# Two residual layers on 32 batches: small products in another order, sums of x on VectorE, sums of weights issued early on GpSimd

## What is computed

```python
def L0(x, weight, bias, lora_a, lora_b, scaling, adapter_id):
    base = jnp.einsum('bsi,oi->bso', x, weight) + bias
    low = jnp.einsum('bsi,bri->bsr', x, lora_a[adapter_id])
    return base + scaling[adapter_id][:, None, None] * jnp.einsum('bsr,bor->bso', low, lora_b[adapter_id])

def L1(x, weight, adapter_ids):
    return jnp.einsum('bij,bkj->bik', x, weight[adapter_ids])

x = x + L0(x, ...)      # x (32, 128, 2048), weight (2048, 2048)
x = x + L1(x, ...)      # weight (16, 2048, 2048), one of 14 used by each batch
```

## Time and profile before

| | |
|---|---|
| median of 3 runs | 2782.98 us (2781.64 to 2783.62) |
| the profiled execution, its own time | 2777.48 us |
| its span in the profile | 2775.7 us |
| mean granted clock of TensorE | 0.972 |
| TensorE busy in matmuls | 2603.3 us (94% of the span) |
| VectorE busy | 2257.2 us (81%) |
| ScalarE busy | 1392.5 us (50%) |
| GpSimd busy | 1100.5 us (40%) |
| plain DMA queue | 649.46 MB, 65.4% of 16 engines |
| accumulating DMA queue | 33.56 MB, 6.4% |

### The profile page before, as it was taken

How to read it: one execution, slowest core, us unless ns; L and a number is a source line. 1 busy time by engine, 2 the same in 40 slices (tenths; PEclk the granted TensorE clock), 3 DMA queues, 4 the chain that set the end, 5 groups by cost and what they waited for, 6 DMA issues and landing times.

```text
span 2775.7 us, 35408 instructions
## 1 busy us (share of the span) xinstructions
PE 2603.3 (94%) x12154; PEld 2132.6 (77%) x12154; DVE 2257.2 (81%) x1902; ACT 1392.5 (50%) x1486; POOL 1100.5 (40%) x718
## 2 busy tenths in 40 slices
PE   7886998899998989998999999999999999999999
PEld 5665787677877777776888888888878878878887
DVE  7877799998887899887878888777877877867865
ACT  3322333333433333335666666666666756756665
POOL 7647477764446687551032041130320311301402
PEclk9998999999999999999999999999999999999999
DMA  5786764354366544656877768768799999998996
GB/s 217 303 298 233 227 182 137 116 187 167 122 206 212 176 134 167 191 207 240 287 259 277 266 222 309 243 237 284 248 351 325 334 352 338 321 349 302 312 320 234
DMA packets 213715, 686.32 MB, mean 247 GB/s; under 512 B 23424, under 2 KB 31648, under 8 KB 213536
## 3 DMA queue, kind: packets, MB, share of 16 engines
q1 hardware_dynamic: 204032, 649.46, 65.4%
q0 software_dynamic: 9216, 33.56, 6.4%
q10 hardware_dynamic: 288, 1.05, 0.1%
HBM read 650.42 MB, written 100.66 MB: 271 GB/s over the span
## 4 chain that ended last, share of the span: by engine, by line
PE 66%; DVE 16%; DMA 7%; issue 6%; POOL 3%; SPq 1%; ACT 1%; DVEq 0%; POOLq 0%; ACTq 0%
PE acc L1195 16%; PE acc L1196 16%; PE acc L1197 16%; PE acc L1112 6%; PE acc L1114 6%; PE acc L1113 6%; DVE tx L1067 5%; DVE ws L1067 5%; DVE xb L987 3%; DMA wb<-w 2%; DVE acc L1057 2%; DMA xb<-x_sums 2%; DMA xb<-x 1%; PE acc L1151 1%; DMA acc<-w 1%
## 5 line engine op out<-in xcount | busy, mean ns | idle before, releaser
L1067 DVE TENSOR_TENSOR ws<-wb,ws 128x1024 fp32r<-128x1024 f32 x964 | 1312.0, 1389 | 300.8 <-ACT ws L923 288.0
L923 ACT CAST ws<-wb 128x1024 fp32r<-128x1024 f32 x964 | 985.9, 1050 | 992.6 <-PE acc L1197 421.8
L1195 PE MATMUL acc<-ws,ops 128*128 128x512 f32 (+1 forms) x2048 | 804.2, 393 | 30.7 <-DVE lows L1017 17.8
L1196 PE MATMUL acc<-ws,ops 128*128 128x512 f32 (+1 forms) x2048 | 800.9, 391 | 0.0
L1197 PE MATMUL acc<-ws,ops 128*128 128x512 f32 (+1 forms) x2048 | 800.1, 391 | 0.0
L829 POOL TENSOR_TENSOR wb<-wb,eye_s 128x128 f32<-128x128 f32 x384 | 316.9, 855 | 1206.2 <-DMA wb<-w 1205.9
L1112 PE MATMUL acc<-tx,ws 128*128 128x512 f32 x1568 | 635.7, 405 | 132.7 <-DVE tx L1067 66.5
L1113 PE MATMUL acc<-tx,ws 128*128 128x512 f32 x1568 | 627.2, 400 | 0.0
L1114 PE MATMUL acc<-tx,ws 128*128 128x512 f32 x1568 | 627.0, 400 | 0.0
L1112 PEld LDWEIGHTS acc<-tx,ws 128*128 128x128 f32 x1568 | 305.6, 195 | 218.2 <-DVE tx L1067 80.5
L1195 PEld LDWEIGHTS acc<-ws,ops 128*128 128x128 f32 x2048 | 386.7, 189 | 112.1 <-DVE lows L1017 19.1
(11 more groups left out here) (64 smaller groups left out, 1249.4 us busy)
## 6 DMA issues: line engine op xcount, KB each, us to landing
wb<-w SPq DMA_DIRECT2D x816, 512.0 KB, 7.7
xb<-x SPq DMA_DIRECT2D x78, 512.0 KB, 5.5
wb<-w_sums SPq DMA_DIRECT2D x64, 512.0 KB, 7.0
xb<-x POOLq DMA_DIRECT2D x64, 512.0 KB, 8.7
y<-acc SPq DMA_DIRECT2D x32, 1024.0 KB, 8.1
out<-ost SPq DMA_DIRECT2D x128, 256.0 KB, 7.3
xst<-xt SPq DMA_DIRECT2D x60, 512.0 KB, 6.6
ystage<-y SPq DMA_DIRECT2D x60, 512.0 KB, 11.0
```

Source lines behind the costliest of these rows:

```text
L923: eng.copy(hi, src).then_inc(s_hi, 1)
L1067: eng.tensor_tensor(lo, src, hi, ALU.subtract).then_inc(s_lo, 1)
L1195: eng.matmul(dst, yh, wh, start=begin, stop=False)
L1196: eng.matmul(dst, yh, wl, start=False, stop=False)
```

## The change

The steps of a product come in another order. By the table `T_SLOT` the x operands are now b11, b21, t2, t1, t3 (in b12), b22 and t4 (in b21), and the second step is the plain product of b21 and a12. All four x sums are VectorE's (t3 = b22 - b12 is issued two steps before the product begins, t2 = b11 + t3 one step before, t4 and t1 in steps 0 and 1), and GpSimd keeps the weight sums: s1 = a21 + a22 is issued in the last two steps of the product before, s2 = s1 - a11 in steps 0 and 1, s4 and s3 behind. b21 and a12, which were used last, are now the operands of the second step; they are still the last blocks that come free in the product before. Evictions of a step are all issued at its end, z and w go to VectorE. Of the four sums of big weight blocks only two remain in DRAM (one VectorE operation per tile, 16 in all); products 3, 4 and 5 get their weights by an accumulating DMA ("wacc"), like x. Identity is added in four products of seven, not six. The LA blocks stand two steps earlier. The number of matmuls is the same.

```diff
-X_NEXT = {"b11": "b22", "b12": "b12", "b22": "b21", "b21": "b11"}
-W_NEXT = {"a11": "a21", "a21": "a11", "a22": "a12", "a12": "a22"}
-X_FREE = {"b11": 3, "b12": 4, "b22": 5, "b21": 6}
-W_FREE = {"a11": 3, "a21": 4, "a22": 5, "a12": 6}
-T_SLOT = ("b11", "b11", "b11", "b22", "b12", "b21", "b11")
-W_SLOT = ("a11", "a21", "a21", "a21", "a11", "a12", "a22")
+X_NEXT = {"b22": "b11", "b12": "b12", "b11": "b22", "b21": "b21"}
+W_NEXT = {"a21": "a21", "a22": "a11", "a11": "a12", "a12": "a22"}
+X_FREE = {"b22": 3, "b12": 4, "b11": 5, "b21": 6}
+W_FREE = {"a21": 3, "a22": 4, "a11": 5, "a12": 6}
+T_SLOT = ("b11", "b21", "b11", "b11", "b12", "b22", "b21")
+W_SLOT = ("a11", "a12", "a11", "a21", "a11", "a12", "a22")
...
-W_PLAIN = {0: (0, 0), 1: (0, 1), 6: (1, 1)}
-W_SUM = {2: 0, 3: 1, 4: 2, 5: 3}
-UNIT = (1, 0, -1, 2, 1, 2, 1)
+W_PLAIN = (("w", 0, 0), ("w", 0, 1), ("d", 0), ("d", 0), ("w", 0, 0), ("d", 0), ("w", 1, 1))
+W_ADDED = {3: ("w", 0, 0), 4: ("w", 1, 0), 5: ("d", 1)}
+UNIT = (1, 0, -1, 0, 1, 0, 1)
...
-        return te[at["W", s, ot]] + 0.5
+        return te[at["W", s, 3]] + 0.4 + 0.1 * ot
...
+        if n in W_ADDED:
+            for role in W_ROLE:
+                for h in range(2):
+                    adds.append((lo_key("W", s0 - K + W_FREE[role], h) + 9.0, "wacc", (q, role, h)))
         for h in range(2):
-            adds.append((lo_key("W", s0, h) + 1.3, "s3", (q, h)))
-            adds.append((lo_key("W", s0, h) + 4.0, "s1", (q, h)))
-            adds.append((lo_key("W", s0 + 1, h) + 1.3, "s2", (q, h)))
-            adds.append((lo_key("W", s0 + 2, h) + 1.3, "s4", (q, h)))
+            adds.append((past(s0 - 2 + h, 0.3) if q else -8.5 + 4.0 * h, "s1", (q, h)))
+            adds.append((past(s0 + h, 0.3) if q else lo_key("W", 0, h) + 8.0, "s2", (q, h)))
+            adds.append((past(s0 + 1 + h, 3.0 if h == 0 else 2.9), "s4", (q, h)))
+            adds.append((past(s0 + 2 + h, 0.3), "s3", (q, h)))
         for c in range(2):
-            sums1.append((lo_key("T", s0, c) + 2.0, "t1", (q, c)))
-            sums2.append((lo_key("T", s0 + 1, c) + 2.0, "t2", (q, c)))
-            adds.append((lo_key("T", s0 + 1, c) + 5.0, "t3", (q, c)))
-            adds.append((lo_key("T", s0 + 2, c) + 4.0, "t4", (q, c)))
+            sums.append((past(s0 - 2, 8.0 + 0.1 * c) if q else -12.0 + c, "t3", (q, c)))
+            sums.append((past(s0 - 1, 8.0 + 0.1 * c) if q else -9.0 + c, "t2", (q, c)))
+            sums.append((past(s0, 8.0 + 0.1 * c), "t4", (q, c)))
+            sums.append((past(s0 + 1, 8.0 + 0.1 * c), "t1", (q, c)))
...
+                if kind == "wacc":
+                    q, role, h = index
+                    eng.wait_ge(s_wb[WS[q][role]][h], 16 * (q + 1))
+                    eng.dma_start(w_tile(q, role, h), w_source(eng, q, role, h, W_ADDED[q % K]),
+                                  accum_op=ALU.add).then_inc(s_wa[WS[q][role]][h], 16)
+                    continue
...
+                    if what == "t3":
+                        x_saved(eng, q, "b12", c)
+                        x_ready(eng, q, "b12", c)
+                        x_ready(eng, q, "b22", c)
+                        ins = eng.tensor_tensor(b12, b22, b12, ALU.subtract)
+                    elif what == "t2":
+                        eng.wait_ge(s_lo, number["T", K * q, c] + 1)
+                        eng.wait_ge(s_sum, sum_no["t3", q, c])
                         x_saved(eng, q, "b11", c)
-                        x_ready(eng, q, "b12", c)
...
+                        ins = eng.tensor_tensor(b11, b11, b12, ALU.add)
```

More of the change, by code:

```diff
@@ L69, in slots_of @@
     return slots
[L72 removed]
+XS = [slots_of(("b11", "b12", "b21", "b22"), X_NEXT, q) for q in range(NG * K)]
 WS = [slots_of(("a11", "a12", "a21", "a22"), W_NEXT, q) for q in range(NG * K)]
@@ L235, in program, with past @@
         raw_user[k], free_at[k] = what, key + 1.5
-    adds, sums1, sums2 = [], [], []
+    def past(s, after):
+        return max(t_of(s), -12.0) + after
+    adds, sums = [], []
     for q in range(NG * K):
```

312 lines of the change are left out of this document (141 added, 171 removed).

## The result

| | before | after |
|---|---|---|
| median of the runs (us) | 2781.68 (2775.8 to 2783.62, 8 runs) | 2766.12 (2762.2 to 2772.58, 8 runs) |
| profiled execution: span (us) | 2775.7 | 2760.7 |
| first layer, 98 steps (us) | 1264.4 | 1246.4 |
| GpSimd busy (us) | 1100.5 | 790.6 |
| accumulating queue (MB, share) | 33.56, 6.4% | 58.73, 10.8% |

The ratio is 0.9949, 95% interval 0.9936 to 0.9963: faster by half a per cent, 15.6 us. The forecast was 2684, with a range from 2612 to 2745, so the result lies outside it; the sign was right and five sixths of the gain are missing. The second layer is not where they went: the span less the first layer's windows is 1511.3 before and 1514.3 after.

A forecast was written before the change was run, and what follows sets the result against it. Bound: a chain of sums made in turns on VectorE and GpSimd. First layer: product 0 97, product 1 79, twelve others 914, plus losses, gives 1165 us against 1264, 99 less: 2684, range 2612 to 2745.

The forecast's parts named there:

- The opening: First layer's start: step 3 near 66, 7 later than now; product 0 takes 97 us, bounds 88 and 105.
- Product 2: Waits for saves cost 5 us in each group; in the first group 7 more for `made` tiles.
- The prices of a plain and an accumulating tile: While product 3 loads: 1.36 us a plain tile, 2.64 an accumulating one, scaled to 1.3 and 2.55.
- D: Slower: GpSimd waits in order, accumulates land one after the other, products 3 and 4 take 133 us each; 2864, chance 0.06.
- B: Queues and double buffers absorb the extra 20 us of copies: gain 166 us, 2617; chance 0.22.
- Rival C: GpSimd's sums slip into VectorE's splits, VectorE bounds at 80 us a product: 25 us, 2709; chance 0.12.
- Rival E: Sums come no earlier, t3 and s1 wait for late tiles, only product 1 gains: 48 us, 2735; chance 0.05.
- products 3 and 4: Late second steps in each group: product 3 loses 16 us (bounds 5 and 28), product 4 loses 8 (0 and 20).
- Products 5 and 6 at 1 each: Products 5 and 6 of each group lose 1 us each, 4 in all.
- Turns costed at nothing: GpSimd's 112 weight sums cost 2.1 us each, 235 in all, if meeting VectorE; taken as falling beside evictions, costing nothing.
- The estimate from the same page: By the skill's page, 48 more accumulate issues cost 2.5 us each, 120 us of GpSimd's time; left out of the sum.
- Product 1 at 79: Big product 1 loses its ping-pong, 48 tile moves for `made` fit beside its loads: 79 us, bounds 76 to 95.

The follow-up runs named there:

- e1: The changed kernel without its 48 accumulating weight loads (products 3, 4 and 5 take the plain tile alone): 2703.53 us, 0.9736 of the kernel before.
- e7: The changed kernel with GpSimd's s1, s2 and s3 also waiting for the end of the step before: 2752.14 us, 0.9906 of the kernel before.
- e5: The changed kernel with t3 one step later in VectorE's order: 2779.36 us, 1.0006 of the kernel before.
- e3: The changed kernel with plain loads only, no accumulating loads of x or weights and no saves: 2661.42 us, 0.9577 of the kernel before.
- e11: The changed kernel with every accumulating transfer of x and weights made plain, same sources, queue and waits: 2678.70 us, 0.9628 of the kernel before.
- e6: The changed kernel with x and weights loaded in order of use, first sums moved into the product itself: 2813.78 us, 1.0121 of the kernel before.
- e15: The changed kernel with only x loaded in order of use, t3 and t2 behind the second step's low halves: 2747.72 us, 0.9891 of the kernel before.
- e2: The changed kernel without the 32 saves of x sums and their waits: 2740.78 us, 0.9870 of the kernel before.
- e10: The changed kernel with the edits of e8 and e7 together: 2690.72 us, 0.9683 of the kernel before.
- e14: The changed kernel with the edits of e8 and e7 and the x order of e15: 2719.51 us, 0.9790 of the kernel before.
- e8: The changed kernel with all four weight sums made once in the opening and read from DRAM, no weight accumulates: 2721.71 us, 0.9787 of the kernel before.

## Why the prediction was wrong

*What held.* The opening: product 0 at 101.9 us for 97 (bounds 88 and 105), with step 3 at 62.1 where 66 was said. Product 2 lost 15.3 us in the first group and 4.7 in the second for 12 and 5. Products 0 and 1 of the second group took 77.2 and 76.2. The prices of a plain and an accumulating tile came out at 1.40 and 2.63, unscaled, where the earlier trace rows give 1.36 and 2.64. GpSimd waits for base tiles as D says, but landings overlap (one every 3.8 us though each takes 10 to 11), so D is out, and so is B: the copies are not hidden, e1 gets 60 us back by leaving out 48 of them.

*Rival C was half right.* Over the last twelve products VectorE is busy for 892 of 1049.7 us, 85%, but that mean hides where it bounds. In product 5 of the first group it is busy for 80.60 of 81.70 us, and C had said that a product would need 80. With GpSimd's sums held (e7) the same product takes 76.2 us, VectorE busy for 73.86. So C's loss is real in some products; it is not the large one.

*Rival E had the nearest number, 2735, by luck.* It said that only product 1 would gain; six others gained 6 to 14 us each, and products 3, 4 and 6 paid them back. Its reason holds for little: VectorE stood idle 51.9 us ahead of t3, 39.2 of that for saves and 12.7 for tiles, and e5 shows that starting t3 early was still worth 0.6%.

*The step that failed first: products 3 and 4.* The first layer took 1246.4 us where the sum said 1165: 81 us are missing. Products 3 and 4 are the largest part, 37.5 us; product 6 is 21, product 1 some 9, product 5 some 7, product 0 is 5. The sum gave product 3 a loss of 16 us and product 4 one of 8 in each group; they lost 22.7 and 21.3, then 21.9 and 19.6. I read the engines' share and the tile's price rightly, and then asked for the landing of the *last* tile (product 4) and for the save of t2's tile (product 3), and put the loss at the second step. The tile that decides is b11: third loaded, but wanted first, and its weight operand a11 is third too. An x pair with its weight pair takes 7.6 us of full engines where an x pair with a plain weight tile took 5.1, and b11 waits for both kinds of the two roles ahead of it. The share of 0.95 to 0.98 before hid this, because it rises no further when more is queued: what it leaves out is the backlog, visible only in the time to landing of a base tile (6 to 11 us before, 19 to 26 after, in the stretches that load products 3 and 4). Shown by e1, e3 and e11 (amount) and by e6 and e15 (order). What the forecast did say, a wait for saves at the second step of product 3, is there with 5.50 us, and e2 takes it away.

*Products 5 and 6 at 1 each.* They lost 5.5 and 13.8, and in the second group 3.8 and 15.2 (with LA and the hand-over, where 7 was said). Product 5's 5.5 are gone in e7 (76.2 us), where nothing but the turns was touched, and also in e1 (76.7); the second group's 3.8 stay in e7 (81.5) and go in e1 (76.6). Product 6 of the first group takes 90.0 us here, 91.6 in e1, 86.4 in e11, 85.0 in e7 and 82.0 in e3: it owes some to the turns and some to its x transfers, nothing to the accumulates of weights. y stores of 1 MB run among them. No run took these alone, so the split isn't known.

*Turns costed at nothing.* The working named a price of 2.1 us each if GpSimd's sums met VectorE's, and took the low end because they should fall beside evictions. They meet t2, t1 and low parts instead: GpSimd starts when a low part is written, which is when VectorE goes on to its next operation. VectorE was busy for 1044.4 us in the first layer, where the low end was 899 and the high end 1134. What the hold gave is 14 us in e7 (12 by the ratios) and 31 in e10, a lower bound for the turns, since it only moves them. The right form of the term was the one of rival C, added to the forecast and not set against it. The turn itself, 1.22 and 2.40 becoming 3.4 for both, fits what the Trainium skill's page "SBUF — State Buffer", section "SBUF: two separate sides", states for a VectorE operation with two SBUF inputs beside a GpSimd one that reads SBUF: whoever comes first holds the shared ports for its whole instruction. The trace agrees: in e14 two VectorE sums took 6.76 us beside two GpSimd sums of 3.34 and 3.38. The estimate from the same page that I set beside the sum (48 issues stretched by 2.5 us) isn't seen: the added issues take 872 ns in the mean for 32 of them and 877 for 16. It was the wrong sentence to draw on: the page states it for a two-port operation, and the same section says that `tensor_tensor`, which these sums and low parts are, has no two-port mode.

*Product 1 at 79.* It took 94.8, the upper bound; 6.42 of these are TensorE's gap ahead of product 2's first step, so product 1's own time is 88.4, 9 more than said. That the 48 tile moves "fit beside its loads" is likely the wrong part: e8, with twice as many sums, gives 108.7. But e8 also has 40 VectorE operations for them instead of 16, so traffic and VectorE's share are not parted.

*The range.* Its upper end took products 3 and 4 at their bounds, and E. It let every other term stand at its middle, though four of them (products 1, 5 and 6 and the turns) could err in the same direction: a wait that is removed uncovers all of them at once.
